# Dense stages of a fused graph network in seven chunks, with transposed products, on one NeuronCore

## The chip, the cores and the metric
The kernel runs on 1 core of a Trainium2 chip. The metric is the device time of one launch in microseconds. Before the change the median of three runs was 4432.37 us (4431.76 to 4432.81). The engines: TensorE (PE) multiplies and transposes, VectorE (DVE) and ScalarE (ACT) work on elements, GpSimd (POOL) issues the indirect DMAs that gather and scatter rows, SyncE (SP) issues the plain DMAs.

## The reference
Four graph networks are applied in sequence to one graph of N = 3125 nodes (128 features, fp32) and E = 50000 edges. Each takes the layer-normalized, rectified state of the nodes, and its result is added to the state `x`. Six times rows of a table over the nodes are gathered by each edge's source and summed at its target:

- L0 (a GCN with batch norm): `h = relu(bn(x @ fc_w + fc_b))`, and twice `z = relu(bn(A(h) @ conv_w[i] + conv_b[i])); h = z + h`, where `A` sums `w_e * dinv[target] * dinv[source] * h[source]` over a node's edges. Passes 0 and 1. `bn` takes mean and variance over all nodes, per feature.
- L1 (attention, 4 heads): `h = n @ W_node.T`, edge scores from `h[src]`, `h[tgt]` and the edge's attributes, leaky ReLU, softmax over each target's edges, sum. Pass 2.
- L2 (attention, 8 heads): `q, k, v = h @ Wq + bq, ...`, softmax, sum, then `@ Wo + bo`. Pass 3.
- L3 (two layers): `h = h @ Wt.T + bt`, a gate `tanh(h[src] @ Wg + bg)` by node, `out = A'(gate * h) + h`. Passes 4 and 5; ReLU after each.

## The kernel before, in words
The nodes lie in 25 blocks of 128 (NB = 25, the last has 53 nodes): `X` and `HN` are [128 lanes, 25, 128] tiles, nodes on the lanes. The edges are sorted by target into 416 tiles of 128, in 52 groups of 8. A gather pass (`sum_pass` or `part_pass`) runs over the groups: GpSimd issues eight indirect gathers a group (L468) from a table in DRAM into a ring of 4 groups (8 in the attention passes), TensorE multiplies them by one-hot matrices (L891), VectorE adds the results into `ACC` (L1301). GpSimd's program for a pass begins with a wait for the table's stores (L455, 32 = two DMAs).

Between the passes stand the dense stages. They are eight in number, 0 to 7: 0, 1 and 2 are the products with `fc_w` and `conv_w`, 3 is `W_node`, 4 is q, k, v, 5 is `Wo`, 6 and 7 are `Wt`. Each works on all nodes at a time:

- VectorE makes the input in `HN` over all 25 blocks: `layernorm` (L1178: statistics, subtraction of the mean, ReLU and scale), or the sum of a pass weighted by degree (L1508), or the division by the softmax's denominators (L1473).
- TensorE transposes the 25 blocks (L747); ScalarE copies them from PSUM to `FT` (L498), feature on the lanes. One counter of banks (`chunk`, `evac`) alternates between banks 0 and 1 for everything, four blocks a bank.
- TensorE multiplies. In stages 0 to 2 `product_T` keeps the weights in the array and moves 512 nodes (L757); the bias is added in ScalarE's copy. In stages 3 to 7 a block of `FT` is the stationary operand and the weights move (L767, L994, L1005), with a second matmul over one row of ones to add the bias (L768, L1006). A product starts when the last transposed block is copied (`pe.wait_ge(s_ev_chunk, chunks[0])`).
- In stages 0 to 2 batch norm follows: statistics on VectorE (L1491), scale and ReLU of the whole tensor on ScalarE (`answer`, L573), the residual sum (L1501), and 25 transposes back.
- In stages 6 and 7 VectorE multiplies by `Wg` and reduces (L1540, L1541), ScalarE takes tanh, and VectorE scales the table (L1544).
- When the whole table is ready, `s_table` rises and SyncE stores it with two DMAs (L414 for 24 blocks, L415 for the last one).

Each engine works through its own program in order; the order is the text's. The engines meet only at semaphores. `link` makes an engine wait for its own last instruction, `ask` sends a root or an exponential to ScalarE (L1037) and waits for it.

Of the kernel before, what the change touches and what calls it, by code (L numbers as in the profile page):

```python
# [8 lines left out]
ALU = mybir.AluOpType  # L9
ACT = mybir.ActivationFunctionType  # L10
# [102 lines left out]
def gnn_kernel(nc, x, src, dst, edge_attr, edge_weight, fc_w, fc_b, conv_w, conv_b, bn_gamma, bn_beta,  # L113
               W_node, W_edge, a_vec, Wq, bq, Wk, bk, Wv, bv, Wo, bo, Wt, bt, Wg, bg, out):
    ctx = ExitStack()
    with ctx:
# [58 lines left out]
        cols = sb("cols", [P, 9])  # L175
        brow = sb("brow", [1, 6, D])
        wgb = sb("wgb", [P, 2, D])
# [122 lines left out]
        s_pe_chunk = sem("s_pe_chunk")  # L300
        s_ev_chunk = sem("s_ev_chunk")
# [61 lines left out]
        def bcast(ap, shape):  # L363
# [7 lines left out]
        L1_CH = [(c, min(3, NB - 3 * c)) for c in range((NB + 2) // 3)]  # L371
        STAGES = [("wT", 2), ("T", 7), ("Z", 7), ("T", 7),
                  ("T", 7), ("Z", 7), ("T", 7),
                  ("T", 7), ("Z", 7), ("T", 7),
                  ("T", 7), ("L1", len(L1_CH)),
                  ("T", 7), ("QKV", NB),
                  ("T", 7), ("O", 7),
                  ("T", 7), ("O", 7),
                  ("T", 7), ("O", 7)]
        CH0 = [sum(n for _, n in STAGES[:k]) for k in range(len(STAGES) + 1)]  # L380


        @block.sync
        def _(sp):
# [25 lines left out]

            for k in range(len(PASSES)):
                sp.wait_ge(s_table, k + 1)
                t = TABS[k]
                sp.dma_start(tab_dram[k][0:(NB - 1) * P, :].rearrange("(b p) f -> p b f", p=P), t[:, 0:NB - 1, :]).then_inc(s_stored[k], 16)  # L414
                sp.dma_start(tab_dram[k][(NB - 1) * P:N, :], t[0:TAIL, NB - 1, :]).then_inc(s_stored[k], 16)  # L415
# [13 lines left out]
            sp.wait_ge(s_table, len(PASSES) + 1)  # L429
            sp.dma_start(out[0:(NB - 1) * P, :].rearrange("(b p) f -> p b f", p=P), X[:, 0:NB - 1, :]).then_inc(s_out, 16)  # L430
            sp.dma_start(out[(NB - 1) * P:N, :], X[0:TAIL, NB - 1, :]).then_inc(s_out, 16)
            sp.wait_ge(s_out, 32)
            for k in range(len(PASSES)):
                sp.wait_ge(s_stored[k], 32)
# [3 lines left out]
        def _(pool):  # L438
# [15 lines left out]
            for k in range(len(PASSES)):  # L454
                pool.wait_ge(s_stored[k], 32)  # L455
# [18 lines left out]
        def _(act):  # L474
            done = [0]
            chunks = [0]
# [8 lines left out]
            for k, v in enumerate([bq, bk, bv, bo, bt[0], bt[1]]):  # L485
                act.dma_start(brow[:, k, :], v.rearrange("(o f) -> o f", o=1)).then_inc(s_load_w, 16)
            for k in range(2):
                act.dma_start(wgb[:, k, :], Wg[k].rearrange("(o f) -> o f", o=1).broadcast_to([P, D])).then_inc(s_load_w, 16)
# [7 lines left out]
            def evac(dst_ap, src_ap, func=ACT.Copy, **kw):  # L496
                act.wait_ge(s_pe_chunk, chunks[0] + 1)
                nc.scalar.activation(dst_ap, src_ap, func, **kw).then_inc(s_ev_chunk, 1)  # L498
                chunks[0] += 1

            def bank_of():
                return bank[chunks[0] % 2]

            def transposes(to):
                for c, n in T_CH:
                    evac(to(c, n), bank_of()[:, 0:n * P])

            def feat(c, n):
                return FT[:, c * 512:c * 512 + n * P]

            def back(c, n):
                return HN[:, 4 * c:4 * c + n, :].rearrange("p b f -> p (b f)")


# [170 lines left out]
            for c, n in enumerate([4, 3]):  # L685
                evac(wT[:, 4 * c:4 * c + n, :].rearrange("p b f -> p (b f)"), bank_of()[:, 0:n * P])
            root(); root()
            root()
            transposes(feat)
            for layer in range(3):  # L690
                for c, n in T_CH:
# [887 lines left out]
```

## Time and profile before

| What | Value |
|---|---|
| Median of three runs | 4432.37 us |
| The profiled execution's own time | 4432.22 us |
| Its span | 4430.4 us, 48122 instructions |
| TensorE busy | 1947.8 us (44%) |
| VectorE busy | 2251.4 us (51%) |
| ScalarE busy | 1094.4 us (25%) |
| GpSimd busy | 2777.1 us (63%) |
| Mean granted TensorE clock | 0.652 of full speed |

The busy times are sums over the whole span, in which passes and dense stages alternate. GpSimd's busy time is the issue of gathers: 2496 of them in the passes (L468), some 0.95 us each with 0.3 between them, and 400 scatters of edge records at the beginning. A row of a timeline gives start, length, engine, line, operation, tiles, and in brackets how long the engine had been idle and who released it. The name `pool` among the tiles is the kernel's scratch `pool2`, in which `FT` lies; `arena` holds `ZT`, `HT`, `TAB` and `QKV`.

### The profile page before, as it was taken

Reading aid. Unit: us, or ns where it says so; the run is one execution under the profiler, and the core shown is the slowest. Engines: PE = TensorE matmul, PEld = TensorE weight load, DVE = VectorE, ACT = ScalarE, POOL = GpSimd, SP = SyncE. Lnnn points to the kernel's source line nnn. Section 1 sums busy time; section 2 is a strip of 40 time slices with the busy share of each in tenths; the row PEclk is TensorE's granted clock in tenths of the full one; section 3 lists DMA queues with packets and bytes.
Section 4 is the critical chain, followed back from the end, with each engine's and each line's share of the span. In section 5 each row is a group of like instructions: output and inputs, shape, how many; then the busy total and the mean of one; then the engine's idle time right before and its main releaser. Section 6 shows DMA issues by size and latency. Waiting matters only on the chain. (4 is left out here: it accounts for less than half of the span.)

```text
span 4430.4 us, 48122 instructions
## 1 busy us (share of the span) xinstructions
PE 1947.8 (44%) x10480; PEld 1717.4 (39%) x10507; DVE 2251.4 (51%) x5375; ACT 1094.4 (25%) x3112; POOL 2777.1 (63%) x2902
## 2 busy tenths in 40 slices
PE   7521006666433333457665445554443333433332
PEld 7411005555333333346564244544333333333332
DVE  8672027777554444346666358878523333333333
ACT  2101002222300000367775257776200000000000
POOL 0677767777467776177773077775037777177775
PEclk9997556666665556665566767777556655565555
DMA  4100012222221223133332144444011222211223
GB/s 126 37 3 3 3 38 53 53 53 52 31 57 53 52 52 48 49 76 82 79 81 31 49 129 129 129 128 85 1 38 53 53 53 52 28 52 52 53 53 51
DMA packets 145729, 254.66 MB, mean 57 GB/s; under 512 B 57658, under 2 KB 81503, under 8 KB 145300
## 3 DMA queue, kind: packets, MB, share of 16 engines
q0 software_dynamic: 99328, 193.52, 19.0%
q1 hardware_dynamic: 40058, 46.93, 3.7%
q10 hardware_dynamic: 6170, 12.57, 0.9%
q14 instruction: 145, 1.19, 0.1%
q8 instruction: 28, 0.46, 0.0%
HBM read 236.52 MB, written 16.30 MB: 57 GB/s over the span
## 5 line engine op out<-in xcount | busy, mean ns | idle before, releaser
L468 POOL DMA_INDIRECT pool<-tab_dram,tblk x1248 | 1181.8, 947 | 735.9 <-issue 379.3
L891 PE MATMUL bank<-pool 128*128 128x128 f32 x3328 | 769.6, 425 | 1522.5 <-DMA pool<-tab_dram,tblk 1037.5
L891 PEld LDWEIGHTS bank<-pool 128*128 128x128 f32 x3328 | 718.0, 327 | 1565.7 <-issue 1119.9
L468 POOL DMA_INDIRECT arena<-tab_dram,tblk x832 | 798.6, 960 | 508.0 <-DMA tab_dram<-arena 254.4
L1301 DVE TENSOR_TENSOR ACC<-ACC,bank 128x128 f32 x1664 | 476.8, 287 | 987.7 <-PE bank L891 774.5
L449 POOL DMA_INDIRECT rec_dram<-arena,ACC x400 | 394.3, 986 | 233.4 <-issue 120.1
L468 POOL DMA_INDIRECT pool<-tab_dram,arena x416 | 401.7, 966 | 141.1 <-issue 126.1
L944 PE MATMUL bank<-pool 128*128 128x136 f32 (+1 forms) x1664 | 308.6, 356 | 52.9 <-DVE pool L1374 34.2
L498 ACT ACTIVATE pool<-bank 128x512 f32<-128x512 f32 (+1 forms) x56 | 29.8, 551 | 1177.2 <-PE bank L747 1176.9
L944 PEld LDWEIGHTS bank<-pool 128*128 128x128 f32 x1664 | 292.4, 257 | 61.8 <-DVE pool L1374 37.8
L1431 DVE TENSOR_TENSOR ACC<-ACC,pool 128x132 f32 (+1 forms) x832 | 248.2, 298 | 119.2 <-DVE ACC L1431 5.8
L559 ACT ACTIVATE arena<-bank,key 128x128 bf16<-128x128 f32 x416 | 146.3, 377 | 643.8 <-PE bank L834 643.8
L618 ACT ACTIVATE pool<-iota,recS 128x128 f32<-128x128 f32 x832 | 252.8, 387 | 0.0
L920 PE MATMUL bank<-HN,pool 128*128 x832 | 155.5, 363 | 111.8 <-DVEq L1339 89.5
L920 PEld LDWEIGHTS bank<-HN,pool 128*128 128x128 f32 x832 | 143.6, 269 | 125.4 <-issue 125.4
L917 PEld LDWEIGHTS bank<-at,pool 128*128 128x128 f32 x832 | 158.9, 293 | 38.8 <-issue 38.8
L917 PE MATMUL bank<-at,pool 128*128 x832 | 158.5, 323 | 31.4 <-issue 15.7
L929 PE MATMUL bank<-ident,sg 128*128 128x128 f32 x52 | 23.1, 445 | 329.2 <-DVE lm L1363 323.2
L1197 DVE TENSOR_TENSOR pool<-bank,recS 128x1024 f32<-128x1024 f32 x104 | 127.3, 1224 | 71.4 <-issue 71.3
L1262 DVE TENSOR_SCALAR pool<-bank,arena 128x128 f32<-128x128 f32 x416 | 137.3, 401 | 39.8 <-issue 39.8
L1262 DVE TENSOR_SCALAR pool<-bank,recS 128x128 f32<-128x128 f32 x416 | 137.2, 401 | 39.9 <-issue 39.9
L929 PEld LDWEIGHTS bank<-ident,sg 128*128 128x128 f32 x52 | 9.6, 184 | 339.5 <-issue 288.9
(251 smaller groups left out, 3183.7 us busy)
## 6 DMA issues: line engine op xcount, KB each, us to landing
pool<-dst_dram SPq DMA_DIRECT2D x104, 256.0 KB, 3.5
pool<-tab_dram,tblk POOLq DMA_INDIRECT x1248
arena<-tab_dram,tblk POOLq DMA_INDIRECT x832
HN<-in_edge_attr_dram ACTq DMA_DIRECT2D x23, 500.0 KB
pool<-tab_dram,arena POOLq DMA_INDIRECT x416
rec_dram<-arena,ACC POOLq DMA_INDIRECT x400, 2.1
tab_dram<-arena SPq DMA_DIRECT2D x4, 1536.0 KB
tab_dram<-arena SPq DMA_DIRECT2D x1, 3072.0 KB
```

The costliest lines, as they stand in the source:

```text
L449: nc.gpsimd.indirect_dma_start(rec_dram, bass.IndirectOffsetOnAxis(ap=row_all[:, c:c + 1], axis=0), rec_all[:, c, :], None).then_inc(s_sca ...
L468: nc.gpsimd.indirect_dma_start(to[:, j, :], None, tab_dram[k], bass.IndirectOffsetOnAxis(ap=idx[:, G * g + j:G * g + j + 1], axis=0)).then ...
L559: nc.scalar.activation(signs[:, half, j, :], bank[j // 4][:, (j % 4) * P:(j % 4 + 1) * P], ACT.Sign, scale=-1.0, bias=key[:, bass.ds(G * g ...
L618: nc.scalar.activation(OHF[:, half, j, :], iota[:, 0:P], ACT.Square, scale=-1.0, bias=one[:, R_DST:R_DST + 1]).then_inc(s_osq, 1)
L891: last = nc.tensor.matmul(bank[4 + 2 * (q % 2) + j // 4][:, (j % 4) * P:(j % 4 + 1) * P], OH[:, q, j, :], rows[:, q, j, :], start=True, st ...
L917: last_ = nc.tensor.matmul(bank[4 + half][:, 4 * j:4 * j + 4], OHT[:, half, j, :], at4[:, bass.ds(vals[j], 1), :].rearrange("p b h -> p (b ...
L920: last_ = nc.tensor.matmul(bank[4 + j // 4][:, (j % 4) * P:(j % 4 + 1) * P], OHT[:, half, j, :], hn1[:, bass.ds(vals[j] * D, D)], start=Tr ...
L944: last_ = nc.tensor.matmul(bank[j // 3][:, (j % 3) * ww:(j % 3 + 1) * ww], OHF[:, half, j, :], weighed[k][:, half, j, :], start=True, stop ...
L1197: return v.tensor_tensor(to, (iota[:, 0:P] if k in HEADS else iota_p).unsqueeze(1).to_broadcast([P, G, P]), records(k)[:, bass.ds(G * g, G ...
L1262: v.tensor_scalar(OH[:, q % RING, j, :], iota_p, one[:, R_DST:R_DST + 1], one[:, R_W:R_W + 1], ALU.is_equal, ALU.mult).then_inc(s_ohw, 1)
L1301: v.tensor_tensor(acc, acc, bank[4 + 2 * (q % 2) + j // 4][:, (j % 4) * P:(j % 4 + 1) * P], ALU.add).then_inc(s_acc, 1)
L1431: v.tensor_tensor(acc, acc, own[:, j, 0:sw], ALU.add).then_inc(s_sum, 1)
```

## The change
The stages 0 to 7 run in seven chunks of four blocks (the last of one) down the engines. A helper `flow` interleaves the steps of a stage on each engine: in slot s a step with lag l works on chunk s - l. The shared counters of chunks and banks give way to one semaphore per kind of step; transposes alternate between banks 0 and 1, products between 4 and 5, products with few columns between 2 and 3, transposes back between 6 and 7 (q, k, v: 4 to 7). All products but q, k, v have the weights as stationary operand and 512 nodes moving; the bias is added in ScalarE's copy into `ZT`, and the result is transposed back. q, k and v lose their bias matmul; VectorE adds the bias as it reads the bank. The normalization itself moves from VectorE to ScalarE, one block at a time, with roots taken in two halves (HALF = 4 chunks). The gate's product with `Wg` becomes a matmul with one column. Tables and the output are stored by one DMA per chunk, and GpSimd waits for all seven.

```diff
+        HALF = 4
+        def flow(*lanes):
+            for slot in range(CHUNKS + max(lag for lag, _ in lanes)):
+                for lag, work in lanes:
+                    if 0 <= slot - lag < CHUNKS:
+                        work(*T_CH[slot - lag])
 @block.sync
             for k in range(len(PASSES)):
-                sp.wait_ge(s_table, k + 1)
-                sp.dma_start(tab_dram[k][0:(NB - 1) * P, :]..., t[:, 0:NB - 1, :]).then_inc(s_stored[k], 16)
-                sp.dma_start(tab_dram[k][(NB - 1) * P:N, :], t[0:TAIL, NB - 1, :]).then_inc(s_stored[k], 16)
+                for c, n in T_CH:
+                    if k == 3:
+                        sp.wait_ge(s_kv, 4 * c + n)
+                    else:
+                        sp.wait_ge(s_table, CHUNKS * (k if k < 3 else k - 1) + c + 1)
+                    store(tab_dram[k], TABS[k], s_stored[k], c, n)
 @block.gpsimd
-                pool.wait_ge(s_stored[k], 32)
+                pool.wait_ge(s_stored[k], 16 * CHUNKS)
 @block.scalar
+            def normed(b):
+                nc.scalar.activation(HN[:, b, :], X[:, b, :], ACT.Relu, scale=stat[:, 4, b:b + 1], bias=stat[:, 5, b:b + 1]).then_inc(s_normed, 1)
+            def norm(stage):
+                def work(c, n):
+                    if c in (0, HALF):
+                        act.wait_ge(s_norm, 2 * LNS[stage] + (1 if c == 0 else 2))
+                    for q in range(n):
+                        normed(4 * c + q)
             for layer in range(3):
+                    flow((0, turned(layer)), (1, made(layer, cols[:, layer:layer + 1])))
...
-                answer(HT if layer == 0 else FT[:, :], ZT, ACT.Relu, scale=bnv[:, 5:6], bias=bnv[:, 6:7])
-                transposes(back)
+                for c, n in T_CH:
+                    nc.scalar.activation(to[:, c * 512:c * 512 + n * P], ZT[...], ACT.Relu, scale=bnv[:, 5:6], bias=bnv[:, 6:7]).then_inc(s_relu, 1)
             root()
+            flow((0, norm(3)), (1, turned(3)), (1, only(0, root)), (2, made(3)))
...
+            flow((0, norm(4)), (1, turned(4)), (1, only(0, root)))
...
+            flow((0, turned(5)), (1, made(5, cols[:, 9:10])))
             root()
+            flow((0, norm(6)), (1, turned(6)), (1, only(0, root)), (2, made(6, cols[:, 10:11])), (3, gates(6)))
+            flow((0, turned(7, ACT.Relu)), (1, made(7, cols[:, 11:12])), (2, gates(7)))
 @block.tensor
+            for layer in range(3):
+                flow((0, turn(layer)), (1, make(layer, wfc[:, layer, :])))
+                flow((0, back(layer)))
+            flow((0, turn(3)), (1, make(3, wT[:, 0, :])), (1, side(3, FT, ust[:, :], 8)), (2, back(3)))
+            flow((0, turn(4)), (1, products))
+            flow((0, turn(5)), (1, make(5, wT[:, 4, :])), (2, back(5)))
             for layer in range(2):
-                product_bias(wT[:, 5 + layer, :], brow[:, 4 + layer, :])
+                flow((0, turn(6 + layer)), (1, make(6 + layer, wT[:, 5 + layer, :])),
+                     (2, side(6 + layer, ZT, cols[:, 12 + layer:13 + layer], 1)), (2, back(6 + layer)))
 @block.vector
-            def layernorm():
+            def norm_stats(c, n):       # bn_stats and bn_aggr of the chunk's blocks
...
+                if c + 1 == HALF:
+                    norm_ask(0, 4 * HALF)
+                elif c + 1 == CHUNKS:
+                    norm_ask(4 * HALF, NB)
+                if c == HALF:
+                    norm_answer(0, 4 * HALF)
+                elif c + 1 == CHUNKS:
+                    norm_answer(4 * HALF, NB)
...
+                    flow((0, weighted_nodes), (3, channel_stats))
...
+                    flow((0, residual(1)), (2, table_by_degree(1)))
+                    flow((0, residual(2)), (2, add_to_x(2)))
+            flow((0, head_table))
+            flow((0, add_divided))
+            for b in range(NB):
+                dve.wait_ge(s_qkv, b + 1)
+                v.scalar_tensor_tensor(HN[:, b, :], bank[4 + b % 4][:, 0:D], 0.25, bqkv[:, 0, :], ALU.mult, ALU.add).then_inc(s_q, 1)
+                v.tensor_tensor(QKV[:, b, D:3 * D], bank[4 + b % 4][:, D:3 * D], bqkv[:, 1:3, :]..., ALU.add).then_inc(s_kv, 1)
+            flow((0, lambda c, n: divided(c, n).then_inc(s_nodes, 1)), (3, add_to_x(5)))
+            flow((0, gated_table(6)))
+            flow((0, next_nodes), (3, gated_table(7)))
+            flow((0, result))
```

`make` is one matmul of up to 512 columns; `turn` and `back` are four transposes; `side` is four matmuls with 8 columns (stage 3: the attention scores) or 1 (stages 6 and 7: the gate). `made` and `turned` are ScalarE's copies. `gated_table` copies the chunk to `HN`, forms the gate's weight, and scales the chunk into `TAB`.

## Rows read from the trace of the kernel before

**Rows 1.** The page's first line.
```profile
span 4430.4 us, 48122 instructions
```

**Rows 2.** Timelines of POOL: start, length, instruction, in brackets the wait before.
```profile
643.81 0.97 POOL L468 DMA_INDIRECT pool<-tab_dram,arena  x1 [14.65 <-DMA tab_dram<-arena]
...
1238.39 4.14 POOL L468 DMA_INDIRECT pool<-tab_dram,tblk  x1 [66.50 <-DMA tab_dram<-arena]
...
1856.72 0.94 POOL L468 DMA_INDIRECT arena<-tab_dram,tblk  x1 [95.84 <-DMA tab_dram<-arena]
...
2539.73 0.94 POOL L468 DMA_INDIRECT arena<-tab_dram,tblk  x1 [158.52 <-DMA tab_dram<-arena]
...
3273.52 0.95 POOL L468 DMA_INDIRECT pool<-tab_dram,tblk  x1 [206.09 <-DMA tab_dram<-arena]
...
3876.82 0.94 POOL L468 DMA_INDIRECT pool<-tab_dram,tblk  x1 [84.06 <-DMA tab_dram<-arena]
```

**Rows 3.** Timelines of DVE: the first dense operation behind each pass.
```profile
1191.22 3.49 DVE L1508 TENSOR_TENSOR HN<-ACC,dinv_in 128x3200 f32<-128x3200 f32 x1
...
1775.91 3.49 DVE L1508 TENSOR_TENSOR HN<-ACC,dinv_in 128x3200 f32<-128x3200 f32 x1
...
2454.08 3.49 DVE L1477 TENSOR_TENSOR HN<-ACC 128x3200 f32<-128x3200 f32 x1
...
3151.78 3.49 DVE L1477 TENSOR_TENSOR HN<-ACC 128x3200 f32<-128x3200 f32 x1
...
3807.42 3.49 DVE L1547 TENSOR_TENSOR pool<-ACC,dinv_out 128x3200 f32<-128x3200 f32 x1
...
4410.96 3.49 DVE L1547 TENSOR_TENSOR pool<-ACC,dinv_out 128x3200 f32<-128x3200 f32 x1
```

**Rows 4.** Timeline ahead of pass 0, DVE.
```profile
638.39 0.53 DVE L1269 CAST arena<-arena 128x416 uint32<-128x416 f32 x1 [247.48 <-DMA arena<-rec_dram]
```

**Rows 5.** Timelines of DVE: layer norm in D, its requests in B and C.
```profile
1821.64 0.18 DVE L1186 TENSOR_SCALAR stat<-stat 128x25 f32<-128x25 f32 x1
...
2467.89 0.18 DVE L1186 TENSOR_SCALAR stat<-stat 128x25 f32<-128x25 f32 x1
...
3200.07 4.93 DVE L1181 BATCH_NORM_STATS2 M<-X 128x6 f32<-128x128 f32 x25
...
3206.83 0.18 DVE L1186 TENSOR_SCALAR stat<-stat 128x25 f32<-128x25 f32 x1
```

**Rows 6.** Timelines of DVE and ACT: batch norm in A and B.
```profile
1207.28 4.59 DVE L1491 BATCH_NORM_STATS2 bnst<-arena 128x6 f32<-128x512 f32 x7 [12.57 <-ACT arena L498]
...
1213.60 3.05 ACT L573 ACTIVATE pool<-arena,bnv 128x3200 f32<-128x3200 f32 x1 [0.87 <-DVEq L1039]
...
1799.01 3.05 ACT L573 ACTIVATE pool<-arena,bnv 128x3200 f32<-128x3200 f32 x1 [0.87 <-DVEq L1039]
```

**Rows 7.** TensorE: timelines of A and D, and line 995 (min/median/max ns).
```profile
1200.47 6.20 PE L757 MATMUL bank<-pool,wfc 128*128 128x512 f32 x14 [0.37 <-ACT pool L498]
...
3155.38 5.74 PE L747 MATMUL bank<-ident,HN 128*128 128x128 f32 x25 [24.58 <-DVEq L1533]
...
3171.54 0.80 PE L767 MATMUL bank<-wT,pool 128*128 128x128 f32 x2
...
3172.99 0.80 PE L767 MATMUL bank<-wT,pool 128*128 128x128 f32 x2
...
L995 PE MATMUL bank<-ust,pool x50: 175/216/256, 1835.5 to 1846.3; 128*128 128x8 f32 x50
```

**Rows 8.** Timeline of ACT in pass 2.
```profile
1903.27 0.97 ACT L618 ACTIVATE pool<-iota,recS 128x128 f32<-128x128 f32 x3
```

**Rows 9.** Windows of B and D: length, busy PE, PEld, DVE, ACT, POOL; clock; DMA.
```profile
1836.00:1847.00 11.00, 10.52 (x96) 10.43 (x94) 0.12 (x1) 4.31 (x9) 0.00 (x0) 1.00 0.00 0
3171.00:3181.00 10.00, 10.00 (x29) 6.86 (x29) 0.00 (x0) 1.19 (x2) 0.00 (x0) 0.50 0.01 2
```

**Rows 10.** DMA issues: KB each, median us from issue to landing.
```profile
wedge<-in_L_gnn_W_edge_dram SPq DMA_DIRECT2D x2, 32.0 KB, 3.7
```

More of the change, by code:

```diff
@@ L494, in link @@
                 act.wait_ge(s_act, done[0])
[L496 to L509, printed above, removed]
@@ new lines, in gates, with work, only @@
+            def gates(stage):
+                def work(c, n):
+                    g = before(stage, c, SIDE)
+                    act.wait_ge(s_side, g + 1)
+                    nc.scalar.activation(stat[:, 6, 4 * c:4 * c + n], bank[2 + g % 2][:, 0:n], ACT.Tanh,
+                                         bias=bgb[:, stage - 6:stage - 5]).then_inc(s_side_read, 1)
+                return work
+            def only(chunk, work):
+                return lambda c, n: work() if c == chunk else None
@@ new lines, in back, with work @@
+            def back(stage):
+                def work(c, n):
+                    g = before(stage, c, MADE)
+                    if stage == 0:
+                        pe.wait_ge(s_relu, c + 1)
+                    elif stage < 3:
+                        pe.wait_ge(s_hadd, CHUNKS * (stage - 1) + c + 1)
+                    else:
+                        pe.wait_ge(s_zt, g + 1)
+                    if g >= 2:
+                        pe.wait_ge(s_taken, g - 1)
+                    of = HT if stage < 3 else ZT
+                    for q in range(n):
+                        last = nc.tensor.transpose(bank[6 + g % 2][:, q * P:(q + 1) * P], of[:, (4 * c + q) * P:(4 * c + q + 1) * P], ident[:, :])
+                    last.then_inc(s_back, 1)
+                return work
@@ L855, in edge_tables @@
             def edge_tables():
-                pe.wait_ge(s_ev_chunk, chunks[0])
                 pe.wait_ge(s_dcol, 1)
@@ L989, in _ @@
-            transposes(node)
-            pe.wait_ge(s_ev_chunk, chunks[0])
-            for c, n in L1_CH:
-                def fill(b):
-                    for q in range(n):
-                        nc.tensor.matmul(b[:, q * AW:q * AW + D], fblock(3 * c + q), wT[:, 0, :], start=True, stop=True)
-                        last = nc.tensor.matmul(b[:, q * AW + D:(q + 1) * AW], fblock(3 * c + q), ust[:, :], start=True, stop=True)
-                    return last
-                chunk(fill)
-            need_feat()
@@ L1017, in _ @@
                 sum_pass(4 + layer)
-            assert chunks[0] == CH0[-1]
         @block.vector
```

403 lines of the change are left out of this document (227 added, 176 removed).

## The prediction
> **What bounds the kernel now.** I read the page's head first, then GpSimd's waits, then the timelines of the stretches between the passes. The profiled execution spans 4430.4 us [rows 1]; its own time was 4432.2 us, so 1.8 us lie around the span, and the median of the three timed runs, 4432.4, is the same within 0.2. GpSimd issues every gather and stood waiting ahead of each of the six passes until a table was stored, 625.7 us in the six rows together [rows 2]. These are the places where the change can act. A pass lasts as long as its gathers: pass 1 starts at 1238.4 and its last gather ends 95.8 before 1856.7, so at 1760.9, which is 522 us for 416 gathers.
>
> Not all of a wait is a dense stage. Behind the last gather the products and sums of a pass still run. So I measure each stretch from the first dense operation on VectorE [rows 3] to GpSimd's restart [rows 2]: A (to pass 1) 1191.22 to 1238.39, 47.2; B 1775.91 to 1856.72, 80.8; C 2454.08 to 2539.73, 85.7; D 3151.78 to 3273.52, 121.7; E 3807.42 to 3876.82, 69.4; and the tail from 4410.96 to the span's end, 19.4. Together 424.2 us. Nothing else can shorten the kernel, as the passes are not edited. The wait ahead of pass 0 (14.65) stands behind the records: VectorE had waited 247.48 for them when they came [rows 4], long after it had made table 0, so stage 0 counts for nothing; the store of its table runs beside the records' load now and after.
>
> Inside a stretch the engines now take turns: VectorE works on whole tensors (3.49 each), TensorE transposes 25 blocks in 5.74, then multiplies, ScalarE copies, and each waits for the last block of the one before.
>
> **Prices.** A chunk has four blocks (512 elements a lane), and seven chunks count as 6.25. VectorE: 0.70 for 512 elements (4.59 for seven pieces, the last short, and 3.49/6.25 plus a start) [rows 3, 6]; the four layer-norm statistics 0.79 (4.93/25 each) and their aggregates 0.3, since 3200.07 to 3206.83 holds 4.93 and 25 aggregates [rows 5]. TensorE: a chunk of transposes 0.92 (5.74/6.25), a 512-column product 1.0 (6.20/6.25), four side products with a few columns 0.88 (216 ns each) [rows 7]. The same product with one block as weights and a bias matmul behind it stepped 1.45 a block in D (3171.54 to 3172.99), 5.8 a chunk [rows 7]; the wide form without bias matmuls is the largest part of this change. ScalarE: 0.6 to copy a chunk, 3.05/6.25 and a start from the row of 3.05 [rows 6]. Its new normalization of a block is priced by the one-hot activations of the same size with a bias column: three in 0.97 [rows 8], 1.3 a chunk; half as much again would still fit under TensorE's slot below. A handoff costs 0.1 to 0.3, which I put at 0.2 a slot.
>
> The clock sets TensorE's prices. In the late part of D's products the granted clock was 0.50 (1.2 GHz), while B's products, also behind 25 transposes, ran at 1.00 (2.4 GHz) [rows 9]. My sum takes the mixed prices above, which come from both; a slot of turn, product, side product and turn back is 3.6, without the side product 2.8. At 1.2 GHz throughout I double the product and the side product: 5.6 and 3.8. That is the upper bound; the lower one is 2.7, as at the other level of the clock the transposes may take half.
>
> **Part by part.**
> A. Weighted nodes, turn and product now overlap. First chunk 0.8, first turn 0.92, then TensorE 1.92 a slot for five slots, 1.3 and 0.3 for the short chunk: 12.9. Copy and statistics of the one-block last chunk 0.6, then the same chain of small operations as now (4.59 after 1207.28 is 1211.87, relu at 1213.60: 1.7) [rows 6]: relu starts 15.2 in, against 22.4 (1191.22 to 1213.60). From relu on, VectorE is the longest: two residual adds ahead and then add plus table at 1.45 a slot, 10.6. The last store is one block (26.5 KB), issued last; the nearest row, a load of 32 KB, landed 3.7 after issue [rows 10]. I take 3.8, since the chunk before it is still moving. A whole table takes 8.9 (4410.96 and three operations of 3.49 is 4421.5; the span ends at 4430.4). So 14.4 against 24.8 (1213.60 to 1238.39). A gains 7.2 + 10.4 = 17.6.
> B. The same start as A: 15.2 against 23.1, gain 7.9. From relu (1799.01) to the second request for roots VectorE does residual, sum, statistics, while its two whole-tensor normalizations (3.49 each) go to ScalarE: 2.7 a slot, 18.9 with the two split requests, against 22.8 (to 1821.82) [rows 5, 6], gain 3.9. One small loss is inside: the root of the second half stands in ScalarE's queue behind the first two chunks' normalization and ahead of the third's, so ScalarE stands until VectorE's seventh chunk. It then has norm, copies and turn for five chunks; TensorE's 3.6 a slot is longer than ScalarE's 2.9. 1.0 + 5 x 3.6 + 3.0 for the last two chunks down the engines + 3.8 store = 25.8, against 34.9 to GpSimd's restart; gain 9.1. B gains 20.9.
> C. Division, sum and statistics chunk by chunk are 17.6 where whole tensors took 14.0 (2454.08 to 2468.07): a loss of 3.6 [rows 4, 5]. Then 71.7 is left now. After: 384-column products without bias are 0.75 (three times 0.25, a quarter of the 512-column one) [rows 7]; four of them and a turn are 3.75 a slot, VectorE's two reads of each bank are 0.7 a block with two starts, just under TensorE. 1.0 + 6.25 x 3.75 + 0.8 + 4.5 for the store of rows twice as long = 29.7. Gain 42.0; C gains 38.4.
> D. Stage 5: the first chunk is back at 8.0 through turn, copy, product, copy, turn; VectorE then needs 2.0 a chunk for sum and statistics and 0.7 for the divisions that remain: 23.0 to the request, against 55.2 (3151.78 to 3207.01). Gain 32.2. Stage 6: 1.0 + 5 slots x 3.7 + the load of tanh's table 1.3 + the last chunks 4.5 + store 3.8 = 29.1, against 66.5. Gain 37.4. Here wgb's product and reduction on VectorE (twice 3.49) go to 25 side products on TensorE. D gains 69.6.
> E. Neighbours and ReLU of a chunk, then the same pipe: first table chunk starts at 8.7, 5 x 3.6, the last two 3.1, store 3.8: 33.6 against 69.4. Gain 35.8.
> Tail. 1.65 a chunk on VectorE, 10.4, and 3.8: 14.2 against 19.4. Gain 5.2.
>
> SyncE now issues 49 stores instead of 14, each behind its own wait; nothing else is queued there except the index rows for passes 2 and 3, which now come earlier after the last chunk. GpSimd waits once per pass as before. What stands behind the stores on VectorE (clearing ACC, comparing, in pass 1 the edge tables) is hidden by the first gather group and the ring of four; it loses 5 us of cover and would cost its excess if the ring ran full, which at 10 us a group it does not.
>
> Sum: 17.6 + 20.9 + 38.4 + 69.6 + 35.8 + 5.2 = 187.5. Span 4242.9, time 4244.7: **4245 us**.
>
> **Rivals.**
> 1. TensorE stays at 1.2 GHz. Every chunk brings it waits, and D's products fell to 0.50 after a dense start [rows 9]. Against: B's mixture held 1.00. Price, slot by slot: A 5, B 5 + 10, C 6.25 x 3.0 = 19, D 7 + 10, E 10: 66 us, 4311. The Trainium skill, "TensorE: Matmul & The Clock Gate", section "HAM oscillation", says that short pieces of matmul with waits between them let the clock drop again and again; by that rule this rival is what happens, and the rows above leave it open.
> 2. The stores don't shorten: the last of seven small stores lands as late as a whole table. Five times 5 us and twice that in C: 33 us, 4278. For it: stores share one queue. Against: [rows 10], 3.7 for 32 KB. The Trainium skill, "DMA: Bandwidth & Descriptors", section "Anatomy of one DMA", gives some 2 us fixed for a DMA (measured for GpSimd's path); as an estimate by that page each tail would be 1.7 shorter than I take, 10 us in all.
> 3. Slower: the in-order queues don't interleave, and each chunk walks the whole chain before the next starts. Adding the prices of one chunk's chain: A 5.8 and 3.2 a chunk, 62 in all; B 132; C 79; D 50 + 69; E 68; tail 14: 474 against 424, so 4481. It decides only if over four fifths of the overlap is lost (187.5 of 237). Against it: every queue is written in slots, two banks per kind of result.
> 4. The gather passes themselves don't change; if they did, the difference would stand in their 522 us each.
>
> **How the numbers follow.** The forecast, 4215 to 4275, has 0.60; rival 1, with half-way cases over 4290, 0.20; rival 2, 0.12; below 4215 (all low bounds: 2.8 a slot, 0.6 on VectorE, a store tail of 3) 0.06; rival 3, 0.02. The range reaches from 4213 to 4300. A difference of 0.2% is what these measurements can tell. Faster 0.97, same 0.01, slower 0.02.
>
> **What would show it.** GpSimd's waits after the change: the restart 237 us in all behind the six starts, D near 52, C near 47, E near 34. Products of 512 columns about 1 us apart when a stage is full, and a granted clock at 1.00 in most of it, else rival 1. Last store to restart under 4 us, else rival 2. Passes of 522 us, rival 4. VectorE longest in stage 5 and in the second half of A, TensorE in stages 3, 4, 6 and 7. I am wrong if the stretches fall by much less than half.

## The result, and the profile after

The changed kernel takes 4222.3 us (median of 4 runs, 4222.2 to 4224.0) against 4432.5 (4431.8 to 4432.8): ratio 0.9523, 95% interval 0.9506 to 0.954. Forecast was 4245. The profiled execution, the page's first line:

```profile
span 4222.2 us, 48387 instructions
```

The span fell by 208.2 us from [rows 1]. GpSimd's first gather of each pass, from its timeline; in brackets is how long it had stood (before: [rows 2]):

```profile
638.09 0.97 POOL L502 DMA_INDIRECT pool<-tab_dram,arena  x1 [14.38 <-DMA tab_dram<-arena]
1213.57 0.94 POOL L502 DMA_INDIRECT pool<-tab_dram,tblk  x1 [47.67 <-DMA tab_dram<-arena]
1811.28 0.94 POOL L502 DMA_INDIRECT arena<-tab_dram,tblk  x1 [75.72 <-DMA tab_dram<-arena]
2452.59 0.94 POOL L502 DMA_INDIRECT arena<-tab_dram,tblk  x1 [117.22 <-DMA tab_dram<-arena]
3112.44 0.94 POOL L502 DMA_INDIRECT pool<-tab_dram,tblk  x1 [130.40 <-DMA tab_dram<-arena]
3672.24 0.94 POOL L502 DMA_INDIRECT pool<-tab_dram,tblk  x1 [40.83 <-DMA tab_dram<-arena]
```

VectorE's first dense instruction of each stretch, from its timeline (before: [rows 3]); instructions of 512 or 128 columns stand where one of 3200 stood:

```profile
1184.73 2.50 DVE L1274 TENSOR_TENSOR HN<-ACC,dinv_in 128x512 f32<-128x512 f32 x4
1750.41 2.50 DVE L1274 TENSOR_TENSOR HN<-ACC,dinv_in 128x512 f32<-128x512 f32 x4
2407.35 0.69 DVE L1336 TENSOR_TENSOR HN<-ACC 128x512 f32<-128x512 f32 x1
3066.46 2.50 DVE L1336 TENSOR_TENSOR HN<-ACC 128x512 f32<-128x512 f32 x4
3646.38 5.00 DVE L1328 SCALAR_TENSOR_TENSOR HN<-ACC,dinv_out,HN 128x128 f32<-128x128 f32 x16
4205.93 1.14 DVE L1328 SCALAR_TENSOR_TENSOR HN<-ACC,dinv_out,HN 128x128 f32<-128x128 f32 x4
```

Start to GpSimd's restart (for the tail: to the span's end) gives the stretches in us, the measure of everything below:

| | A | B | C | D | E | tail | sum |
|---|---|---|---|---|---|---|---|
| before | 47.2 | 80.8 | 85.7 | 121.7 | 69.4 | 19.4 | 424.2 |
| forecast | 29.6 | 59.9 | 47.3 | 52.1 | 33.6 | 14.2 | 236.7 |
| after | 28.8 | 60.9 | 45.2 | 46.0 | 25.9 | 16.3 | 223.1 |

So 201.1 of the 208.2 us came from the stretches. The six passes (restart to next start) together changed by 1.4, and pass 0 begins 5.7 earlier (more on this at the end of the part on the prediction).

### The profile page after: what moved, and what is told of

It is laid out like the page before. It is cut to its first block and busy times, and to the rows that moved or that the text cites. A ratio compares the mean times of both kernels' runs of the same rounds, so it can differ in the third digit from the quotient of the medians.

```text
span 4222.2 us, 48387 instructions
## 1 busy us (share of the span) xinstructions
PE 1867.4 (44%) x10336; PEld 1671.4 (40%) x10363; DVE 2256.1 (53%) x5605; ACT 1111.2 (26%) x3173; POOL 2764.5 (65%) x2902
## 5 line engine op out<-in xcount | busy, mean ns | idle before, releaser
L483 POOL DMA_INDIRECT rec_dram<-arena,ACC x400 | 384.9, 962 | 237.4 <-issue 120.7
```

Source lines behind the costliest of these rows:

```text
L483: nc.gpsimd.indirect_dma_start(rec_dram, bass.IndirectOffsetOnAxis(ap=row_all[:, c:c + 1], axis=0), rec_all[:, c, :], None).then_inc(s_sca ...
```

## The experiments

Not all of the times can be compared with each other: in eight of the twelve runs the kernel before itself took 5397 to 5475 us in place of 4433. There the gathers are slower: in the copy of the changed kernel pass 2 takes 595 us, in e5 819. The stretches hardly know of it: before's A was 47.2, and 47.7 and 47.4 in its two variants there (b1, b2); the changed kernel's tail was 16.2 and 16.3, and 16.3 in its variants e2, e4, e5 and e8 there. The changed kernel itself was not run in that condition. So each experiment is read by its stretches; the ratio beside it is to the kernel before in the same condition. The profiles of one kernel scatter too: a copy of the changed kernel read 219.2 where the first profile read 223.1, and 58.8 against 60.9 in B alone. So differences of the sum under 4 us, and of one stretch up to 2.1, are not taken for effects.

| kernel | A | B | C | D | E | tail | sum | time (ratio, interval) |
|---|---|---|---|---|---|---|---|---|
| a0_after | 28.0 | 58.8 | 44.5 | 46.0 | 25.8 | 16.2 | 219.2 | 4220.7 (0.9524, 0.951 to 0.9539) |
| b1_no_bias | 47.7 | 81.2 | 64.6 | 66.0 | 41.3 | 19.5 | 320.3 | 5373.9 (0.9809, 0.9763 to 0.9855) |
| b2_transposed | 47.4 | 81.9 | 85.6 | 76.9 | 46.4 | 19.5 | 357.6 | 5411.9 (0.9877, 0.983 to 0.9924) |
| e9_all_back | 35.3 | 77.8 | 63.6 | 69.7 | 37.5 | 21.6 | 305.5 | 5269.2 (0.9759, 0.9727 to 0.9791) |
| e1_store_late | 32.7 | 64.6 | 52.1 | 54.2 | 31.3 | 21.7 | 256.6 | 5293.9 (0.9658, 0.9613 to 0.9703) |
| e2_steps_apart | 30.3 | 70.2 | 52.4 | 59.8 | 32.1 | 16.3 | 261.0 | 5301.2 (0.9673, 0.9628 to 0.9718) |
| e3_nodes_whole | 32.8 | 69.4 | 53.5 | 55.3 | 32.6 | 16.2 | 259.8 | 4259.3 (0.9608, 0.9593 to 0.9623) |
| e4_warm | 28.6 | 58.7 | 44.5 | 45.4 | 26.0 | 16.3 | 219.5 | 5241.0 (0.958, 0.9555 to 0.9606) |
| e5_pe_more | 28.1 | 62.3 | 43.9 | 48.1 | 27.2 | 16.3 | 225.9 | 5248.1 (0.9591, 0.9561 to 0.9621) |
| e6_three_asks | 28.5 | 55.6 | 45.8 | 44.2 | 26.7 | 16.3 | 217.1 | 4217.4 (0.9515, 0.9502 to 0.9528) |
| e7_asks_warm | 29.0 | 57.4 | 44.4 | 43.7 | 26.2 | 16.3 | 216.9 | 4216.3 (0.9511, 0.9498 to 0.9524) |
| e8_asks_qkv | 28.3 | 59.2 | 41.9 | 45.9 | 25.9 | 16.3 | 217.5 | 5172.4 (0.9577, 0.9552 to 0.9601) |

**a0_after**, the changed kernel again:

> The changed kernel itself, so that the experiments have it beside them on their own chip. If the dense stretches (first dense VectorE instruction to GpSimd's restart) do not depend on the chip, their sum is again 223 us, within 2, whatever the gather passes do; if a slower chip stretches the dense stages too, the sum is above 230 where the kernel before takes more than 4432.

The sum, 219.2, misses the first case's bounds (221 to 225) by 1.8. As the kernel before took 4433 beside it, it says nothing of the slower condition. It is the second reference for the other runs, as "the copy".

**b1_no_bias**, the kernel before with one matmul a block where two stood (the same in stage 4); the bias is left out of its result:

```diff
-nc.tensor.matmul(b[:, q * P:(q + 1) * P], fblock(4 * c + q), w, start=True, stop=False)
-last = nc.tensor.matmul(b[:, q * P:(q + 1) * P], ones[0:1, :], bias, start=False, stop=True)
+last = nc.tensor.matmul(b[:, q * P:(q + 1) * P], fblock(4 * c + q), w, start=True, stop=True)
```

> The kernel before, without the bias matmuls over a row of ones in stages 4 to 7 (the bias is left out of the result). Theory 1 (the bias matmuls alternating with the products brought the granted clock down in stages 5 to 7): a block falls from 1.45 to about 0.25, 30 us a stage, and q, k, v by 23: 113 us less, 4320. Theory 2 (the clock falls anyway with one block as weights): a block halves, 18 us a stage, and q, k, v by 21: 75 us less, 4357.

**b2_transposed**, the kernel before with stages 5 to 7 multiplied the other way (weights stationary, 512 columns, bias in ScalarE's copy, 25 blocks turned back), still step after step over the whole table, and stage 4 as it was:

```diff
-            transposes(feat)
-            for c, n in T_CH:
-                evac(HN[...], bank_of()[:, 0:n * P])
+            transposes(feat)
+            biased(9)          # FT product copied to ZT with bias=cols[:, 9:10], then turned back
```

> The kernel before with one part of the change alone: stages 5, 6 and 7 take the weights as stationary operand with 512 nodes moving, the bias in ScalarE's copy, and are turned back; no chunks down the engines, whole-table stores. Theory: a product goes from 34 us to 6.2 and the turn back adds 6, so 22 us a stage and 66 together, 4366; the other 140 us of the change then come from the chunks, the stores and q, k, v. Rival (the products' form is most of the gain): under 4300.

TensorE's timeline of D's products in stage 5, first in b1, then in b2 (an fp32 product shows as two instructions, so x50 is 25 blocks and x14 seven chunks):

```profile
4038.36 6.02 PE L767 MATMUL bank<-wT,pool 128*128 128x128 f32 x50 [0.37 <-ACT pool L498]
```

```profile
4063.22 6.20 PE L762 MATMUL bank<-pool,wT 128*128 128x512 f32 x14 [0.64 <-ACT pool L500]
```

And the kernel before at the same place, ahead of the fall of the clock:

```profile
3161.61 0.49 PE L767 MATMUL bank<-wT,pool 128*128 128x128 f32 x2 [0.49 <-ACT pool L498]
3162.03 0.48 PE L768 MATMUL bank<-brow,ones 1*128 1x128 f32 x2
3162.44 0.49 PE L767 MATMUL bank<-wT,pool 128*128 128x128 f32 x2
```

With bias matmuls a block takes 0.83 (3161.61 to 3162.44, the clock at 1.00) and, with the clock at 0.50 [rows 9], 1.45 [rows 7]; without them 6.02 / 25 = 0.24, at 1.00. So the one-row bias matmul costs 0.6 a block, more than the product, and the fall of the clock that much again. b1 takes 103.9 off the sum (its time fell by 101), near the first theory. b2 (-66.6, as expected; its time fell by 63) pays 6.20 for the products, and the turns back. It leaves C at 85.6, and b1's C shows what stage 4's bias matmuls cost there: 85.7 - 64.6 = 21 us. Together 88 us of the 201 come from the two places where the change takes bias matmuls away. The transposed form in itself is no gain in the kernel before: D and E together are 107.3 in b1 and 123.3 in b2, so the turns back give up 16 us of what the bias matmuls had cost. b1 adds no bias at all, though; what adding it in VectorE's copies would cost in stages 5 to 7 was not run.

**e1_store_late**, the changed kernel with its seven stores behind one wait:

```diff
-                for c, n in T_CH:
-                    if k == 3:
-                        sp.wait_ge(s_kv, 4 * c + n)
-                    else:
-                        sp.wait_ge(s_table, CHUNKS * (...) + c + 1)
+                sp.wait_ge(s_table, CHUNKS * (...) + CHUNKS)      # k == 3: s_kv, NB
+                for c, n in T_CH:
```

> The changed kernel, but SyncE issues the seven stores of a table (and of the output) only when its last chunk is ready. Theory (the tail of a stretch is the last store alone, since the earlier ones land beside the computing): A, B, D, E and the tail each grow by the 8.9 of a whole table less the 3.4 to 3.9 measured now, about 5 each, and C by about 10, with rows twice as long; 33 us together, 4255. Rival (the stores were limited by their own rate and gain nothing by an early start): within 5 us of 4222.

The sum rises by 33.5 against the first profile of after (37.4 against the copy). In E the last table operation of after ends at 3669.30 and GpSimd restarts at 3672.24, 2.9 later; in e1 the same takes from 4655.45 to 4663.95, 8.5. VectorE's row of after, then VectorE's and GpSimd's of e1:

```profile
3669.01 0.29 DVE L1319 TENSOR_TENSOR arena<-bank,stat 128x128 f32<-128x128 f32 x1
```

```profile
4655.16 0.29 DVE L1319 TENSOR_TENSOR arena<-bank,stat 128x128 f32<-128x128 f32 x1
4663.95 0.94 POOL L502 DMA_INDIRECT pool<-tab_dram,tblk  x1 [45.63 <-DMA tab_dram<-arena]
```

The tail of each stretch is the last store alone, as the prediction had it; rival 2 is out.

**e2_steps_apart**, the chunks kept, but each engine runs all seven of one step before the next step (ScalarE's second root and stage 3's side products move to fit):

```diff
-            for slot in range(CHUNKS + max(lag for lag, _ in lanes)):
-                for lag, work in lanes:
-                    if 0 <= slot - lag < CHUNKS:
-                        work(*T_CH[slot - lag])
+            for step in sorted({lag for lag, _ in lanes}):
+                for c, n in T_CH:
+                    for lag, work in lanes:
+                        if lag == step:
+                            work(c, n)
```

> The changed kernel, but each engine runs all seven chunks of one step before the next step of a stage (turns, then products, then turns back), with the same chunks, semaphores and matmuls. Theory (interleaving pays where VectorE or ScalarE has work beside TensorE's): stage 5 +6.5, stage 6 +7, stage 4 +5, stage 3 +2, stage 7 +2.5, stages 1 and 2 together +1.5: 25 us, 4247. Rival (TensorE's sum bounds every stage whatever the order): within 5 us of 4222.

**e3_nodes_whole**, the slots kept, but TensorE's first turn of a stage waits for the stage's last chunk (in stages 0, 3, 4 and 6 the lanes of ScalarE behind it move from 1, 2, 3 to 7, 8, 9; those of VectorE behind stages 1, 2, 5 and 7 from 3 to 7):

```diff
-                        pe.wait_ge(s_normed, NB * LNS[stage] + 4 * c + n)
+                        pe.wait_ge(s_normed, NB * LNS[stage] + NB)
                     else:
-                        pe.wait_ge(s_nodes, before(stage, c, NODES) + 1)
+                        pe.wait_ge(s_nodes, before(stage, CHUNKS - 1, NODES) + 1)
```

> In this kernel TensorE starts a stage's first turn only when all seven chunks of the stage's node table are there; stores stay per chunk, products transposed. Theory: the start of TensorE on the first chunk is a gain of its own, and what is lost is the time of the last six chunks of each node table: +3 in each of stages 1, 2 and 5 (VectorE 0.6 a chunk), +8 in each of 3, 4 and 6 (ScalarE's 25 normalizations at 0.41 are 10.3, less the first chunk, and the slot is a little shorter afterwards), +5 in stage 7; together +38 (30 to 46) on the sum of the stretches, 223 to 261. Rival: TensorE's slots carry the stage anyway and catch up, under +15.

e2 cost 37.9 (41.8 against the copy) where 25 was expected, and e3 36.7 (40.6 against the copy; its time is 38.6 above the copy's), as expected. In stages 3, 4 and 6 they share a cause: with the steps apart ScalarE normalizes all chunks before it copies the first. In e2's stage 3 TensorE turns two chunks and then waits 6.76 for that copy; in e3 it waits for all of the normalization. TensorE's first turns there:

```profile
1797.74 1.97 PE L788 MATMUL bank<-ident,HN 128*128 128x128 f32 x8 [11.06 <-ACT HN L531]
```

In e3 TensorE stands 11.06 for 25 normalized blocks. So an early start of the second step is worth about what all of the interleaving is. How far the two overlap is argued from these waits; no run has both edits.

**e9_all_back**: e1's and e2's edits together, and one request for the layer norm's roots in place of two.

```diff
-                if c + 1 == HALF:
-                    norm_ask(0, 4 * HALF)
-                elif c + 1 == CHUNKS:
-                    norm_ask(4 * HALF, NB)
+                if c + 1 == CHUNKS:
+                    norm_ask(0, NB)
+                    norm_answer(0, NB)
```

> Three parts taken back together: stores only when the last chunk is ready, each step's seven chunks before the next step, and one root request per layer norm; what stays of the change is the transposed products with the bias in ScalarE's copy, and pieces of a chunk in place of whole-table instructions. Theory: the parts add up, +33 for the stores, +38 for the steps, +8 to +14 for the request, so the sum is 300 to 310 and the time 4300 to 4310. Rival: they overlap (with the steps apart a late store or a late request delays nothing that was not late already), and the sum stays under 285.

305.5, as expected. In E and the tail, which have no layer norm, the parts add up within 0.1: e1's 5.4 and e2's 6.2 on E's 25.9 give 37.5, and 37.5 was measured. Over the whole sum e1 and e2 make 71.4, which leaves 11.0 of 82.4 for the second request, most of it in B and C; no run isolates that. With this the way from before to after is: 424.2, less 66.6 (b2) and 21 (stage 4's bias, from b1) is 336.6; less 31.1, which no run isolates (work in pieces, normalization on ScalarE, gates as side products), is e9's 305.5; less 82 to 86 for stores per chunk, interleaved steps and the second request is after.

**e4_warm**, dummy transposes of the identity on TensorE ahead of stages 1, 2 and 4 to 7 (12 or 16 each, behind waits that place them in idle time), against the slow first slots:

```diff
+            def warm(times):
+                for _ in range(times):
+                    nc.tensor.transpose(bank[0][:, 0:P], ident[:, :], ident[:, :])
```

> The changed kernel with 16 transposes of the identity (12 ahead of stage 6) into bank 0, read by nobody, on TensorE just ahead of the first turn of stages 1, 2 and 4 to 7, in time in which it was idle. In the changed kernel's trace the first two products of each stage take 1.9 instead of 1.0 and the first turns 1.1 instead of 0.6. Theory (the granted clock is at 1.2 GHz when a stage starts and rises because TensorE works): the first slots are at 2.4 GHz, 1.5 us less in A, B and E, 2.5 in C, 2.5 in D: about 9 us, 4213. Rival (the start is set by handoffs, or the clock does not rise earlier): within 2 us of 4222.

Nothing: 219.5 beside the copy's 219.2. TensorE's timeline at the start of E, e4:

```profile
4585.76 2.71 PE L795 MATMUL bank<-ident 128*128 128x128 f32 x14
4590.26 0.66 PE L788 MATMUL bank<-ident,HN 128*128 128x128 f32 x4 [1.79 <-DVEq L1696]
4591.55 1.12 PE L788 MATMUL bank<-ident,HN 128*128 128x128 f32 x4 [0.63 <-DVEq L1696]
4592.45 1.92 PE L804 MATMUL bank<-pool,wT 128*128 128x512 f32 x2
```

The first turn takes 0.66, but behind short waits the second takes 1.12 and the product 1.92 again, as in after. From 4588.5 to 4590.2, without work, the clock still showed 1.00, and from 4592.4 to 4595.0 it was 0.56. So the filler did raise the clock, but this did not last until the first product. Neither another length nor another place was tried.

**e5_pe_more**, the turns back of stages 3, 6 and 7 done twice, 0.47 us more TensorE work a slot:

```diff
+                    for q in range(n if stage in (3, 6, 7) else 0):
+                        nc.tensor.transpose(bank[6 + g % 2][:, q * P:(q + 1) * P], of[:, ...], ident[:, :])
```

> The changed kernel with the transposes back done twice in stages 3, 6 and 7 (same values, same bank), 0.43 us more of TensorE a chunk. Theory of the prediction (TensorE's slot is the longest in stages 3, 6 and 7): +2.7 us in each of B, D and E, 8 in all, 4230. Rival (ScalarE with its normalizations at 0.41 a block, or VectorE, sets the slot): 0 to 1 in each stage, under 4225.

Against the copy B, D and E rose by 3.5, 2.1 and 1.4, 7 in all; against the first profile by 1.4, 2.1 and 1.3. Three stages of 6.25 chunks at 0.47 would be 8.8 if TensorE alone set the slot. The scatter of one profile leaves it open which it is; E shows that there it is not TensorE alone.

**e6_three_asks**, the roots asked for after chunks 2, 4 and 7:

```diff
-        HALF = 4
+        PARTS = [0, 2, 4, 7]
```

> The layer norm's root is requested after chunks 2, 4 and 7 in place of 4 and 7, so ScalarE's normalization can begin two chunks earlier in stages 3, 4 and 6. Theory: ScalarE stood idle before the first request (1770 to 1781 in stretch B) and its slot sets the rest, so each of B and C loses 4 to 5 us and D, where the request sits in the middle of stage 5, 1 to 3: -11 on the sum, 223 to 212. Rival: VectorE's own answers, now three with a wait each, and the input of later chunks take it back: -3 to +3.

**e7_asks_warm**: e6 and e4 together.

> Three requests as in the run before, and dummy transposes on TensorE ahead of stages 1, 2, 4 to 7, which measured -3.6 on the sum by themselves. Theory: the two add up, 223 to 208, some 14 us or 0.3% below the changed kernel. Rival: the earlier start already hides TensorE's slow first slots, and it equals the run with three requests alone within 1 us.

B fell by 3.2 and D by 1.8 against the copy, C rose by 1.3; the sum fell by 2.1 (6.0 against the first profile) where 11 was expected, and e7 adds nothing (216.9). Of these only B's fall is beyond the scatter. TensorE's timeline shows why C has no gain, first the copy of the changed kernel, then e6:

```profile
2425.64 0.60 PE L788 MATMUL bank<-ident,HN 128*128 128x128 f32 x4
2426.08 2.75 PE L843 MATMUL bank<-wT,pool 128*128 128x384 f32 x8
2428.66 0.60 PE L788 MATMUL bank<-ident,HN 128*128 128x128 f32 x4
```

```profile
2418.93 0.60 PE L788 MATMUL bank<-ident,HN 128*128 128x128 f32 x4
2422.43 5.46 PE L843 MATMUL bank<-wT,pool 128*128 128x384 f32 x8 [2.90 <-DVE arena L1670]
```

TensorE now starts early, but VectorE empties its four banks only when it is done with the statistics; TensorE waits 2.90, and comes back at the slow clock (0.50 from 2422.4 to 2428.0; 5.46 for what takes 2.75).

**e8_asks_qkv**, so, besides e6's edit, VectorE's reads of these banks go into its slots:

```diff
-            flow((0, add_divided))
-            for b in range(NB):
+            flow((0, add_divided), (5, qkv_biased))
```

> Three root requests per layer norm, and in stage 4 VectorE's biased copies of Q, K and V taken into its flow five chunks behind the additions, so that TensorE's banks come free while the layer norm's statistics still run. Theory: with three requests alone TensorE began stretch C 7 us earlier but waited 2.9 us for VectorE's banks and fell back to the slow clock (5.46 for eight products in place of 2.75), so C gained nothing; with the banks freed in time C goes from 44.5 to 40 to 42, B stays at about 56 and D at 44, and the sum is 211 to 214 against 219 to 223 of the changed kernel, its time 4209 to 4215. Rival: the additions and requests that the copies push back cost what the banks give; C stays at 44 to 46 and the time at 4217.

C came to 41.9, as expected, but B and D did not keep what e6 had (59.2 and 45.9), with the same code in these stretches, and the sum of 217.5 missed the expected 211 to 214. The windows of B show the difference (length, busy time and count of PE, PEld, DVE, ACT and POOL, then the granted clock, DMA share and GB/s), first the changed kernel, then its copy, then e6, then e8:

```profile
1785.00:1790.00 5.00, 5.00 (x18) 3.80 (x17) 0.39 (x2) 4.38 (x11) 0.00 (x0) 0.50 0.00 0
1790.00:1795.00 5.00, 5.00 (x31) 3.59 (x30) 0.85 (x3) 3.82 (x9) 0.00 (x0) 0.85 0.05 14
```

```profile
1784.00:1789.00 5.00, 5.00 (x27) 3.49 (x27) 0.00 (x0) 4.70 (x12) 0.00 (x0) 0.79 0.00 0
```

```profile
1780.00:1785.00 5.00, 5.00 (x24) 3.67 (x23) 3.71 (x21) 3.52 (x9) 0.00 (x0) 0.68 0.01 3
1785.00:1790.00 5.00, 4.72 (x34) 3.61 (x33) 1.41 (x6) 4.94 (x14) 0.00 (x0) 1.00 0.11 33
```

```profile
2207.00:2212.00 5.00, 5.00 (x19) 3.97 (x19) 0.39 (x2) 3.85 (x10) 0.00 (x0) 0.50 0.00 0
2212.00:2217.00 5.00, 5.00 (x25) 3.43 (x24) 1.71 (x6) 2.95 (x7) 0.00 (x0) 0.75 0.19 54
```

Stage 3's turns begin in e6 and e8 some 30 us into the stretch. From 35 to 40 us in, e6's clock is 1.00 (2.4 GHz), e8's 0.50 (1.2 GHz) with TensorE busy all the time. With the same code B differs by 3.6 us, the size of what e6 had gained. That this is the clock's doing is argued, not shown, as e8 also ran with the slower gathers. But the clock comes up at different places without that too: in the same stretch of 35 to 40 us the changed kernel has 0.50 and its copy 0.79 (B 60.9 and 58.8), and e7, with quick gathers and e6's requests, 0.50 (1787 to 1792; B 57.4). So e6's gain in B is not told apart from this scatter.

e6's time, 4217.4 (4212.8 to 4221.5), and e7's, 4216.3 (4208.6 to 4223.7), lie below the medians of the changed kernel and its copy (4222.3, 4220.7), but their ratio's interval overlaps the copy's (0.951 to 0.9539): no version here is shown to beat the changed kernel.

## Why the prediction was right, and by how much its terms were off

The mechanism held: the time came out of the stretches, the passes stood (rival 4 is out), the chunks interleave (rival 3 is out), rival 2 is out by e1. The time came out 22.7 us under the forecast: 13.6 from the stretches, 5.7 ahead of pass 0, 1.4 in the passes, and 2.0 between span and median: the profiled execution took 1.8 over its span, as I had it, but the other three runs lie 1.5 to 1.8 below it.

**TensorE's slot was priced at 3.6 and is 2.6.** The 3.6 was added up too low in itself: the prices give 0.92 + 1.0 + 0.88 + 0.92 = 3.72, and for C's slot 3.92 where 3.75 stands, 2 us in the sum. (Rival 2's 33 us are 35 by its own terms.) TensorE's timeline at the start of E, after:

```profile
3647.63 1.12 PE L788 MATMUL bank<-ident,HN 128*128 128x128 f32 x4 [4.73 <-DVEq L1684]
3649.82 1.91 PE L799 MATMUL bank<-pool,wT 128*128 128x512 f32 x2
3652.09 1.02 PE L799 MATMUL bank<-pool,wT 128*128 128x512 f32 x2
3652.95 0.95 PE L813 MATMUL bank<-cols,arena 128*128 128x1 f32 x8
3653.76 0.63 PE L832 MATMUL bank<-ident,arena 128*128 128x128 f32 x4
3654.23 0.60 PE L788 MATMUL bank<-ident,HN 128*128 128x128 f32 x4
3654.67 1.02 PE L799 MATMUL bank<-pool,wT 128*128 128x512 f32 x2
```

The steps between starts are 0.86 for the product, 0.81 for the side products, 0.47 and 0.44 for the two turns: 2.58. My turn of 0.92 came from a row of 25 transposes that began behind 24.58 us of idle time [rows 7], so most of it was run at the slow clock (0.50 from 3155 to 3158, 0.62 to 3161.2); here the first slot, behind 4.73 of idle, shows that price again (1.12 and 1.91), and the third one the fast. The low bound I had named, 2.7, was nearly the value. It made stage 6 24.4 (3088.07 to 3112.44) where I had 29.1, and most of E's 7.7.

**With that, TensorE is not the longest in all of them.** In E's first slots it is VectorE, 2.93 a slot (from the fourth chunk on it waits for TensorE again, 0.81 and 0.76); its timeline:

```profile
3654.43 0.69 DVE L1314 COPY HN<-bank 128x512 f32<-128x512 f32 x1 [3.06 <-PE bank L832]
3656.07 1.14 DVE L1328 SCALAR_TENSOR_TENSOR HN<-ACC,dinv_out,HN 128x128 f32<-128x128 f32 x4
3657.36 0.69 DVE L1314 COPY HN<-bank 128x512 f32<-128x512 f32 x1
```

In stage 3 ScalarE and TensorE nearly tie. A block's normalization takes 0.41 (1.64 for four), not the 0.32 of the one-hots [rows 8]; with two copies of 0.6 ScalarE's slot is 2.7 (1791.94 to 1794.63), while the table's pieces come every 2.58. ScalarE's timeline, then VectorE's:

```profile
1791.94 1.64 ACT L531 ACTIVATE HN<-X,stat 128x128 f32<-128x128 f32 x4
...
1794.13 0.60 ACT L556 ACTIVATE arena<-bank 128x512 f32<-128x512 f32 x1
1794.63 1.64 ACT L531 ACTIVATE HN<-X,stat 128x128 f32<-128x128 f32 x4
```

```profile
1795.41 0.69 DVE L1299 COPY arena<-bank 128x512 f32<-128x512 f32 x1 [1.73 <-PE bank L832]
1797.99 0.69 DVE L1299 COPY arena<-bank 128x512 f32<-128x512 f32 x1 [1.73 <-PE bank L832]
```

B's second half, request to restart, took 27.1 (1784.18 to 1811.28), forecast 25.8. That this is so near is luck. Slots of 2.6 in place of 3.6 should have taken some 5 us off. But TensorE's first slots ran at the slow clock, 4.16 from product to product (1785.34 to 1789.50), so the table's first piece came only at 1792.84, 8.7 behind the request, and the store took 0.7 more than its 3.8. The sum had neither. In C TensorE was the longest, as said: 3.02 a slot (turn and eight pieces, 2425.64 to 2428.66), where I had 3.75; C came 2.1 lower.

**D's stage 5**: 21.6 to the request (3066.46 to 3088.07), forecast 23.0. **A**: 28.8 for 29.6.

**Tail**, 16.3 for 14.2. VectorE's timeline:

```profile
4207.95 1.14 DVE L1328 SCALAR_TENSOR_TENSOR HN<-ACC,dinv_out,HN 128x128 f32<-128x128 f32 x4 [0.16 <-DVE X L1691]
```

A chunk is 2.02 (4205.93 to 4207.95), not 1.65: four 128-column instructions cost 1.14, more than the share of a 512-column one that I had taken.

**Rival 1**, TensorE at 1.2 GHz throughout, did not come, but its start did: the first slots of stages 3 and 7 run at the slow level (1.12 for a turn, 1.91 for a product), and in B the clock came up only behind 1790. By the rows above I estimate this at some microseconds a stretch, not 66 in all. The granted clock was 0.97 to 1.00 in the full part of stages 3, 6 and 7 (0.97 from 1792 to 1806 and from 3094 to 3110, 1.00 from 3653 to 3668), and 0.81 in stage 5 (3066 to 3088), where TensorE was busy for 15.5 of 22 us. The Trainium skill ("TensorE: Matmul & The Clock Gate", section "HAM oscillation") says that waits between short pieces of matmul let the clock drop again and again. The traces agree with it where TensorE had waited, as behind E's 4.73; The rival expected such waits in the full slots too, and there were hardly any (busy for 13.7 of the 15 us from 3653). The sign that I had named for rival 2, under 4 us from the last store to the restart, failed in B and C, though e1 shows that rival to be out. From the last table operation to the restart D and E took 2.9 (3109.50 to 3112.44), A 3.7 (1209.9 to 1213.57), B 4.5 (1806.82 to 1811.28) and C, with rows twice as long, 6.1 (2446.52 to 2452.59), where I had 3.8, and 4.5 in C. The fixed 2 us of the Trainium skill ("DMA: Bandwidth & Descriptors", section "Anatomy of one DMA"), given for GpSimd's path, make an estimate of 2.1 for such a tail: D's and E's 2.9 lie midway between this and my 3.8, the others far from it.

**The part that I had called free.** "Stage 0 counts for nothing" is the step of the prediction that failed, by 5.7 us: pass 0 starts at 636.8 to 638.1 in five profiles of the changed kernel and its variants, and at 643.8 in the one of before. GpSimd stands equally long ahead of it (14.65 and 14.38), but its last record scatter ends at 629.16 before and at 623.72 after. VectorE's and GpSimd's timelines of before show where the time lies:

```profile
351.27 3.49 DVE L1189 TENSOR_TENSOR HN<-X,stat 128x3200 f32<-128x3200 f32 x1
351.45 4.14 POOL L449 DMA_INDIRECT rec_dram<-arena,ACC  x1 [0.30 <-issue]
```

```profile
387.42 3.49 DVE L1505 TENSOR_TENSOR arena<-HN,dinv_in 128x3200 f32<-128x3200 f32 x1 [9.21 <-ACT HN L498]
387.57 4.17 POOL L449 DMA_INDIRECT rec_dram<-arena,ACC  x1 [0.31 <-issue]
```

Three scatters of before take 4.14, 3.58 (at 355.90) and 4.17 us where the others take 0.96, 9.0 us too much, and each coincides with one of stage 0's three whole-tensor instructions on VectorE (351.27, 355.15, 387.42; 3.49 each). The changed kernel has none of these instructions there and no such scatter among its 400. Against these 9.0 us its scatters begin 4.6 later (103.47 for 98.89), for which I have no cause, and GpSimd's two later waits are 1.0 shorter together (14.03 for 14.72, 14.38 for 14.65): that leaves 5.4 of the 5.7. No run gives stage 0 back its whole tensors, so the cause rests on this coincidence; but in b1, where they come at 844.77 and later, behind the last scatter (678), no scatter takes over 2 us.

In the condition with slow gathers the first table itself is late: GpSimd's first gather starts at 892.5 and 893.2 in b2 and b1, with stage 0 as before, and at 873.2 to 876.5 in e4, e5 and e8, with stage 0 as changed. There the change gives 16 to 20 us ahead of pass 0, though these runs were on different chips.

## What to carry to other kernels

Price an operation from a row with the engine in the state that it will be in: a row behind idle time is a cold row, and it sets the first slot, not the steady one. Where engines hand whole tensors on, look first for what is not work at all: here one-row bias matmuls between products cost 104 us (b1), the waits for the last block 37 (e3), and stores that wait for the whole table 33 (e1). A further head start gave little (11 expected, 2 to 6 had): in C the next wait took it. And before work is called free because nothing waits for it, look at what else runs beside it: here whole-tensor instructions on VectorE stood beside scatters four times as long as the others.

## What the runs showed of the hardware

TensorE's clock can fall while the engine has no idle time. In e2's stage 7 (windows, columns as above):

```profile
4653.00:4658.00 5.00, 5.00 (x46) 4.98 (x47) 2.91 (x6) 1.74 (x5) 0.00 (x0) 1.00 0.15 43
4658.00:4664.00 6.00, 6.00 (x32) 6.00 (x31) 4.50 (x10) 0.80 (x3) 0.00 (x0) 0.52 0.48 143
```

TensorE was busy all the 11 us, with one-column side products and turns of 128 columns, and the clock fell from 1.00 to 0.52. The kernel before shows the same in D: busy from 3161.6 on with pairs of product and bias matmul, its clock was 1.00 to 3163.7 and 0.53 from there to 3166.0. The interleaved slots of the changed kernel kept 1.00 for the 15 us from 3653. The same product took 0.24 us a block in a row of its own kind (b1) and 1.45 as one of a pair with a one-row bias matmul at the slow clock. And the kernel before took 4433 us or 5397 to 5475, by nothing that was changed, with stretches A, B and the tail of its two variants there within 1.1 us of its own; one chip showed both (a0, e3, e6 and e7 ran on it beside 4433, e8 and e9 beside 5397).

A scatter that GpSimd issues while VectorE works through a whole-tensor instruction of 3.49 us took 3.58 to 4.17 us in place of 0.96 (the kernel before, three of three).
